# The first expert product in fp32 on two 64-row tiles, in place of fp16 high and low halves

## The reference

```python
x = x + ssm(_ln_c(x))            # 64->168 projection, state per image, layernorm over 128, 128->64
t = tokens(x)
t = t + moe0(_ln_t(t))           # 8 experts 64->128->64, exact gelu, two of them weighted per token
x = x + conv(_ln_c(x))           # channel groups of 8 and a 3x3 neighbourhood of the squares
t = t + moe1(_ln_t(t))           # 8 experts 64->256->64, weights: softmax over the two best

def moe(xf):                     # all experts are computed for all tokens
    for e in range(8):
        h = gelu(xf @ W1[e] + b1[e])
        out = out + w[:, e:e + 1] * (h @ W2[e] + b2[e])
```

## Time and profile before

| | |
|---|---|
| median of 3 runs | 723.12 us |
| span of the profiled execution (its own time) | 721.9 us |
| PE busy | 540.6 us (75%), 3010 instructions |
| DVE busy | 523.5 us (73%), 926 instructions |
| ACT busy | 377.9 us (52%), 440 instructions |
| POOL busy | 283.2 us (39%), 240 instructions |
| chain that ended last | DVE 39%, DMA 22%, PE 15% |

### The profile page before, as it was taken

How to read it: one execution, slowest core, us unless ns; L and a number is a source line. 1 busy time by engine, 2 the same in 40 slices (tenths; PEclk the granted TensorE clock), 3 DMA queues, 4 the chain that set the end, 5 groups by cost and what they waited for, 6 DMA issues and landing times.

```text
span 721.9 us, 8643 instructions
## 1 busy us (share of the span) xinstructions
PE 540.6 (75%) x3010; PEld 214.2 (30%) x3010; DVE 523.5 (73%) x926; ACT 377.9 (52%) x440; POOL 283.2 (39%) x240
## 2 busy tenths in 40 slices
PE   2314674589777988799778978798879786975776
PEld 1213223232323332343224323333333221321312
DVE  3266367868798979887998898889978796466312
ACT  2112712566566656756575657555766464543532
POOL 2122156034534453536362544365245433334013
PEclk9999975699999999999999999999999998998699
DMA  4500600063106230605041503350145005500240
GB/s 67 96 9 1 133 0 0 7 128 87 32 1 134 50 69 15 133 12 108 16 107 27 119 16 72 62 119 16 38 81 117 17 14 106 118 16 0 48 86 15
DMA packets 27834, 41.39 MB, mean 57 GB/s; under 512 B 11792, under 2 KB 19088, under 8 KB 27792
## 3 DMA queue, kind: packets, MB, share of 16 engines
q1 hardware_dynamic: 27152, 38.75, 26.2%
q0 software_dynamic: 640, 2.10, 1.0%
HBM read 38.22 MB, written 2.62 MB: 57 GB/s over the span
## 4 chain that ended last, share of the span: by engine, by line
DVE 39%; DMA 22%; PE 15%; issue 8%; POOL 7%; SPq 5%; ACT 4%; POOLq 0%; DVEq 0%; ACTq 0%
DMA WB<-w_scratch 18%; DVE nacc L1132 6%; PE yP L859 5%; PE hP L844 4%; SPq L402 3%; DMA w_scratch<-wTs 3%; DVE YW L1179 2%; POOL stat_c L486 2%; PE sA L760 2%; DVE xsplit L969 2%; PE sA L770 2%; DVE xcen_b L962 2%; POOL stat_b L486 2%; DVE xnrm L962 1%; DVE xnrm L957 1%
## 5 line engine op out<-in xcount | busy, mean ns | idle before, releaser
L691 ACT ACTIVATE H<-hP,b 128x1024 f32<-128x1024 f32 x192 | 209.2, 1110 | 82.6 <-PE hP L844 81.5
L859 PE MATMUL yP<-H,w 128*64 128x512 f32 x768 | 211.3, 632 | 21.3 <-DVE ACC L1179 19.3
L844 PE MATMUL hP<-xT,w 128*128 128x512 f16 x768 | 209.9, 399 | 4.3 <-ACT H L691 4.3
L556 POOL TENSOR_TENSOR ACC<-ACC,YW 128x512 f32<-128x512 f32 x96 | 125.6, 1313 | 194.6 <-DVE YW L1179 194.5
L844 PEld LDWEIGHTS hP<-xT,w 128*128 128x128 f16 x768 | 65.9, 101 | 145.8 <-issue 84.5
L1179 DVE SCALAR_TENSOR_TENSOR YW<-yP,b,WB 128x512 f32<-128x512 f32 x96 | 71.3, 744 | 34.2 <-PE yP L859 34.2
L859 PEld LDWEIGHTS yP<-H,w 128*64 128x64 f32 x768 | 40.1, 138 | 103.3 <-issue 89.0
L1132 DVE SCALAR_TENSOR_TENSOR nacc<-PAD,taps,nacc 128x256 f32<-128x256 f32 x112 | 60.5, 540 | 3.7
L1179 DVE SCALAR_TENSOR_TENSOR ACC<-yP,b,WB 128x512 f32<-128x512 f32 x32 | 23.1, 746 | 46.9 <-DMA WB<-w_scratch 46.9
L540 POOL TENSOR_SCALAR nrg<-nacc,go_col 128x512 f32<-128x512 f32 x8 | 12.6, 1574 | 68.9 <-ACT nacc L659 68.9
L584 ACT ACTIVATE xsq<-xcen 128x512 f32<-128x512 f32 x24 | 15.0, 626 | 36.1 <-DVE xcen L941 36.0
(11 more groups left out here) (144 smaller groups left out, 761.9 us busy)
## 6 DMA issues: line engine op xcount, KB each, us to landing
WB<-w_scratch SPq DMA_DIRECT2D x32, 1024.0 KB, 9.9
X<-in_x SPq DMA_DIRECT2D x8, 256.0 KB, 12.0
out<-X POOLq DMA_DIRECT2D x8, 256.0 KB, 2.8
H<-in_L_ffn_W SPq DMA_DIRECT2D x2, 512.0 KB, 6.2
H<-in_L_ffn_W SPq DMA_DIRECT2D x2, 256.0 KB, 4.2
w<-in_L_ffn_W SPq DMA_DIRECT2D x1, 512.0 KB, 4.8
w_scratch<-wTs SPq DMA_DIRECT2D x16, 32.0 KB, 1.8
w<-in_L_ffn_W SPq DMA_DIRECT2D x1, 256.0 KB, 4.1
```

What stands on the lines that cost most here:

```text
L556: pool.tensor_tensor(ACC[l][:, cols], ACC[l][:, cols], YW[:, u % 4, :], ALU.add).then_inc(summed, 1)
L691: nc.scalar.activation(H[:, s % RING, :], hP[s % 2][:, :], ACT.Gelu, bias=b1[l][:, e * ch + c:e * ch + c + 1], scale=1.0 / WS)\
L844: mm = nc.tensor.matmul(hP[s % 2][:, hf * HALF:(hf + 1) * HALF], w1[l][:, sp, w, :], xT[l][g % 2][:, hf * HALF:(hf + 1) * HALF], start=(sp ...
L859: mm = nc.tensor.matmul(yP[hf][a * C:(a + 1) * C, :], w2[l][:, (2 * j + a) * ch + c, :], H[:, (2 * ch * j + 2 * c + a) % RING, hf * HALF:( ...
```

## The change

The inputs of the experts and of the gate stay fp32. The normalised tensors of b and d are not cast or split. PE turns two tiles of 128 tokens by 64 channels in one fp32 transpose of 128x128; four of them make xT, now 128x512: the channels of the even tiles on the partitions 0 to 63 and those of the odd tiles on 64 to 127. W1 is loaded by DMA as fp32 on both halves and not split. A slot has two fp32 matmuls, one over the rows 0 to 63 and one over 64 to 127, each into its own half of hP. The gate weights stand as a block diagonal, 8 columns for the upper and 8 for the lower half, and four fp32 matmuls make the logits. Tokens are thus in the order even tiles, odd tiles throughout a layer; the write of wgt and the residual additions take this into account by their access patterns. The loads of the experts' constants wait for the memsets of the gate weights.

The order is the same; eight transposes become four and wait for the normalisation itself, four matmuls of hP become two, and sixteen of the gate four. The core of the diff:

```diff
--- before.py
+++ after.py
...
@@ -168,11 +168,10 @@
         alog = sb("alog", [P, HEADS])
         expa = sb("expa", [P, HEADS])
         dpar = sb("dpar", [P, HEADS])
-        gw_f = [sb(f"gw_f{l}", [P, E]) for l in range(2)]
-        gw = [sb(f"gw{l}", [P, 2, E], F16) for l in range(2)]
+        gw = [sb(f"gw{l}", [P, 2 * E]) for l in range(2)]
         gb = [sb(f"gb{l}", [P, E]) for l in range(2)]
         NC = [E * c for c in CHUNKS]
-        w1 = [sb(f"w1_{l}", [P, 2, NC[l], P], F16) for l in range(2)]
+        w1 = [sb(f"w1_{l}", [P, NC[l], P]) for l in range(2)]
         w2 = [sb(f"w2_{l}", [P, NC[l], C]) for l in range(2)]
         b1 = [sb(f"b1_{l}", [P, NC[l]]) for l in range(2)]
         b2 = [sb(f"b2_{l}", [P, PAIRS]) for l in range(2)]
@@ -200,12 +199,10 @@
         xcen_b = sb("xcen_b", [P, T, C])
         xsq_b = sb("xsq_b", [P, T, C])
         xnrm_b = xcen_b
-        xsplit_b = sb("xsplit_b", [P, T, 2 * C], F16)
         xsplit = sb("xsplit", [P, T, 2 * C], F16)
-        xsplit2 = sb("xsplit2", [P, T, 2 * C], F16)
         stat = {L: sb(f"stat_{L}", [P, 4, T]) for L in "anbcd"}
         xTa = sb("xTa", [P, TOK], F16)
-        xT = [[sb(f"xT{l}_{i}", [P, TOK], F16) for i in range(2)] for l in range(2)]
+        xT = [[sb(f"xT{l}_{i}", [P, HALF]) for i in range(2)] for l in range(2)]
         proj = sb("proj", [P, T, PROJ])
         ctS = sb("ctS", [64, HALF])
         zdt = sb("zdt", [P, 5, T, HEADS])
...
@@ -405,29 +404,27 @@
             load("in", both_halves(win_f, W_in) + [(dtb[:, :], rep(dt_bias)), (alog[:, :], rep(A_log))])
             load("out", [(wout_f[:, :], W_out), (gam_col[:, :], ln_gamma.rearrange("(c o) -> c o", o=1)),
                          (bet_col[:, :], ln_beta.rearrange("(c o) -> c o", o=1)), (dpar[:, :], rep(D_param))])
-            load("experts0", both_halves(gw_f[0], g0_w) + [(gb[0][:, :], rep(g0_b))] + [
-                (w1_f[half * C:half * C + C, 0:NC[0] * P].rearrange("d (e h) -> d e h", e=E),
-                 m0_W1.rearrange("e d h -> d e h")) for half in range(2)] + [
+            sp.wait_ge(zeroed, 7 + E)
+            load("experts0", gate_halves(0, g0_w) + [(gb[0][:, :], rep(g0_b))] + [
+                (w1[0][half * C:half * C + C, :, :], m0_W1.rearrange("e d h -> d e h")) for half in range(2)] + [
                 (b1[0][:, :], m0_b1.rearrange("e h -> h e")), (w2[0][:, :, :], m0_W2.rearrange("e h f -> h e f"))] + [
                 (b2[0][half * C:half * C + C, :], m0_b2.rearrange("(j a) f -> a f j", a=2)[half])
                 for half in range(2)])
             load("conv1", both_halves(taps, gamma_s.rearrange("a b c o -> c (a b o)"))
                  + both_halves(nbias, beta.rearrange("(c o) -> c o", o=1))
                  + both_halves(go_col, gamma_out.rearrange("(c o) -> c o", o=1)) + [(bo_rep[:, :], rep(beta_out))])
-            sp.wait_ge(zeroed, 2)
             gk = gamma_k.rearrange("a b i o -> (a b i) o")
             for half in range(2):
                 for grp in range(8):
                     r = half * C + grp * 8
                     sp.dma_start(mix[r:r + 8, r:r + 8], gk[:, grp * 8:grp * 8 + 8]).then_inc(mix_loaded, 16)
-            load("experts1", both_halves(gw_f[1], g1_w) + [(gb[1][:, :], rep(g1_b)),
+            load("experts1", gate_halves(1, g1_w) + [(gb[1][:, :], rep(g1_b)),
                  (b1[1][:, :], m1_b1.rearrange("e (c h) -> h (e c)", h=P)),
                  (w2[1][:, :, :], m1_W2.rearrange("e (c h) f -> h (e c) f", h=P))] + [
                 (b2[1][half * C:half * C + C, :], m1_b2.rearrange("(j a) f -> a f j", a=2)[half])
-                for half in range(2)])
-            for half in range(2):
-                sp.dma_start(w1_f1[half * C:half * C + C, :].rearrange("d (e h) -> d e h", e=E),
-                             m1_W1.rearrange("e d h -> d e h")).then_inc(w1_loaded, 16)
+                for half in range(2)] + [
+                (w1[1][half * C:half * C + C, :, :].rearrange("d (e c) h -> d e (c h)", e=E),
+                 m1_W1.rearrange("e d h -> d e h")) for half in range(2)])
 
             def spread_weights(l, g):
 
...
@@ -689,7 +687,7 @@
                     c, a = r // 2, r % 2
                     e = 2 * j + a
                     nc.scalar.activation(H[:, s % RING, :], hP[s % 2][:, :], ACT.Gelu,
-                                         bias=b1[l][:, e * ch + c:e * ch + c + 1], scale=1.0 / WS)\
+                                         bias=b1[l][:, e * ch + c:e * ch + c + 1])\
                         .then_inc(gelu_done, 1)
 
             walk(moe, final, ab, cd, ACT_AT)
@@ -706,14 +704,23 @@
                     mm = nc.tensor.transpose(dst[:, t * P:(t + 1) * P], src(t), ident16[:, :])
                 mm.then_inc(tr[L].sem, 1)
 
+            def transposes_in_pairs(L, g, dst, after):
+
+                for sm, v in after:
+                    pe.wait_ge(sm, v)
+                for b in range(4):
+                    mm = nc.tensor.transpose(dst[:, b * P:(b + 1) * P], LN[L]["n"][:, 2 * b:2 * b + 2, :],
+                                             ident32[:, :])
+                mm.then_inc(tr[L].sem, 1)
+
             def gate_product(l, g, ps, src):
+
                 if g == 0:
-                    pe.wait_ge(prep, PREP[f"experts{l}"])
+                    pe.wait_ge(loaded[f"experts{l}"], 16 * LOADS[f"experts{l}"])
                 pe.wait_ge(trS[("b", "d")[l]].sem, trS[("b", "d")[l]].at(g))
-                for t in range(T):
-                    for s in range(2):
-                        mm = nc.tensor.matmul(ps[:, t * E:(t + 1) * E], src[:, t * P:(t + 1) * P], gw[l][:, s, :],
-                                              start=(s == 0), stop=(s == 1))
+                for b in range(4):
+                    mm = nc.tensor.matmul(ps[:, b * 2 * E:(b + 1) * 2 * E], src[:, b * P:(b + 1) * P], gw[l][:, :],
+                                          start=True, stop=True)
                 mm.then_inc(gmm[l].sem, 1)
 
             def gate_transpose(l, g, ps):
@@ -785,8 +792,7 @@
                                                   wout[:, n % 2, :], start=(n == 0), stop=(n == 3))
                     mm.then_inc(omm.sem, 1)
                 elif k == "turn_b":
-                    transposes16("b", g, sA16, lambda t: xsplit_b[:, t, :],
-                                 [a_read(k, g), (ln_lo["b"].sem, ln_lo["b"].at(g))])
+                    transposes_in_pairs("b", g, sA, [a_read(k, g), (ln_v["b"].sem, ln_v["b"].at(g))])
                 elif k == "gate":
                     pe.wait_ge(*a_read(k, g))
                     gate_product(0, g, sA, xT[0][g % 2])
...
@@ -839,11 +844,11 @@
                     j, r = s // (2 * ch), s % (2 * ch)
                     c, a = r // 2, r % 2
                     w = (2 * j + a) * ch + c
-                    for sp in range(2):
-                        for hf in range(2):
-                            mm = nc.tensor.matmul(hP[s % 2][:, hf * HALF:(hf + 1) * HALF], w1[l][:, sp, w, :],
-                                                  xT[l][g % 2][:, hf * HALF:(hf + 1) * HALF],
-                                                  start=(sp == 0), stop=(sp == 1))
+                    for hf in range(2):
+
+                        rows = slice(hf * C, (hf + 1) * C)
+                        mm = nc.tensor.matmul(hP[s % 2][:, hf * HALF:(hf + 1) * HALF], w1[l][rows, w, :],
+                                              xT[l][g % 2][rows, :], start=True, stop=True)
                     mm.then_inc(h_ready, 1)
 
                 unit = y_unit(m, s)
@@ -891,7 +896,9 @@
             v.memset(neg_half[:, :], -0.5).then_inc(zeroed, 1)
             for e in range(E):
                 v.memset(iota_m8[:, e:e + 1], float(e - E)).then_inc(zeroed, 1)
-            dve.wait_ge(zeroed, 5 + E)
+            for l in range(2):
+                v.memset(gw[l][:, :], 0.0).then_inc(zeroed, 1)
+            dve.wait_ge(zeroed, 7 + E)
 
             def split(dst_hi, dst_lo, src):
 
...
@@ -918,15 +923,7 @@
                 elif which == "bias":
                     dve.wait_ge(bias_mm, 1)
                     did(v.tensor_copy(out_bias[:, :], sC[:, 0:C]))
-                elif which == "experts0":
-                    dve.wait_ge(loaded["experts0"], 16 * LOADS["experts0"])
-                    split(gw[0][:, 0, :], gw[0][:, 1, :], gw_f[0][:, :])
-                    split(flat[0][:, 0], flat[0][:, 1], w1_f[:, 0:NC[0] * P])
-                elif which == "experts1":
-                    dve.wait_ge(loaded["experts1"], 16 * LOADS["experts1"])
-                    split(gw[1][:, 0, :], gw[1][:, 1, :], gw_f[1][:, :])
-                    dve.wait_ge(w1_loaded, 32)
-                    split(flat[1][:, 0], flat[1][:, 1], w1_f1[:, :])
+                elif which == "conv1":
                     dve.wait_ge(loaded["conv1"], 16 * LOADS["conv1"])
                     did(v.tensor_scalar(nbias[:, :], nbias[:, :], 1e-6, None, ALU.add))
                 assert steps[0] == PREP[which]
@@ -961,12 +958,9 @@
```

(22 more changed lines are left out.)

35 lines of the change are left out of this document (16 added, 19 removed).

## The result

The changed kernel takes 717.09 us as the median of 20 runs (709.39 to 724.27), the kernel before 723.9 us (20 runs, 722.27 to 730.02). The ratio is 0.9864, 95% interval 0.9843 to 0.9885: 1.4% faster, some 10 us by the ratio and 7 by the medians. The forecast was 707.5 us, with a range of 697 to 719.

A forecast was written before the change was run, and what follows sets the result against it. No engine alone bounds it: DVE and DMA take turns. Span 721.9 - 7.7 (b) - 5.0 (d, steady) - 2.1 (d, last group) - 2.0 (start) + 1.2 (hP) = 706.3; median 1.2 above: 707.5 us, range 697 to 719.

The forecast's parts named there:

- the forecast's own case: Whole kernel: the summed terms hold, 707.5 us, within 702 to 713 us, chance 0.50.
- rival 3: Slow clock falls on the chain in piece 4 of every period: 8 us of gain back, 713 to 718 us, chance 0.10.
- Split of b: In piece 2, YW on DVE begins 1.1 us earlier without the split, in seven groups: 7.7 us gained.
- Piece 2: Steady period, first ACC of layer 1 to wgt of layer 0 (410.71 to 441.15): DVE instruction behind DVE instruction.
- hP in fp32: Two fp32 products of 64 rows per step: 1.06 us, 0.1 more; 12 times on the chain, 1.2 us lost.
- rivals 4 and 5: Row tiles of hP overlap partly (4: 718 to 726 us, chance 0.13) or run one after another (5: 880 us, 0.11).
- piece 4: Steady period, first ACC of layer 0 to next write of layer 1, 14.6 us: gains between 0.2 and 1.7 us.
- Start, -2.0: Start: W1 split of 5.0 us goes, transposes, evacuation and gate product of 3 us replace it: 2.0 us gained.
- Gate, transposes and evacuation: PE's transposes about equal, evacuation about 0.4 us less, gate about 0.4 us more: together zero, bounds +-0.5 us.
- d, steady: Split of d removed in five steady periods: piece 3 keeps its length, piece 4 gains 1.0 us each, 5.0 us.
- piece 3: Steady period, wgt to first ACC of layer 0 (441.15 to 456.77): set by DMA, removing d's split worth zero.
- Last group, -2.1: Last group: the split of d stands on the chain itself, 2.2 us, of which 2.1 go.

The follow-up runs named there:

- e2: The kernel before without the subtraction that makes the low part of b, the cast staying: 720.63 us, ratio 0.9925.
- e12: The changed kernel with only the first two of the four matmuls of each gate product: 711.07 us, ratio 0.9782.
- e4: The changed kernel with each of the four matmuls of the gate product made twice: 734.03 us, ratio 1.0135.
- e6: The changed kernel with the read of layer 0's expert weights (WB) cut to a tiny piece from the second group on: 696.61 us, ratio 0.9615.
- e10: The changed kernel with POOL's product Yd held until DVE has written Vs: 723.81 us, ratio 0.9977.
- e7: The changed kernel with nine fp16 matmuls, result unread, put in pauses of PE to keep it busy: 715.36 us, ratio 0.9828.

## Why the prediction was right, and where it was wrong

The direction and the range held; the point was some 7 to 10 us too low. The result lies outside the 702 to 713 us of the forecast's own case and within the 713 to 718 of rival 3, which had a chance of 0.10 and whose mechanism, more slow clock in every steady period, is not what the steady periods show. That the range took it in is in part luck.

By stretches, the profile has 12.3 us more than the 706.3 of the sum, in three nearly equal parts. Up to the write of layer 1, group 0, the terms give 3.1 us and 0.9 was lost; in the five periods they give 10.0 and 6.1 came; behind them they give 2.5 and 1.9 was lost.

- **Split of b, 7 x 1.1 us: right.** YW starts 1.67 us behind the start of the normalisation, 2.85 before: 1.18. Piece 2 is 31.5 to 30.3 us in the trace. Its subtraction alone (e2) gives 5 us.
- **hP in fp32, 1.06 us a step: right** in its size, 1.05. The rivals 4 and 5 fell: two row tiles run side by side as two column tiles do (1.05 us for both, 1.10 for one full product), even writing all 128 partitions each. The count of the steps was too low: the sum had one hP step on the chain in each piece 4, and the chain of the change at 452.11 to 467.78 has four, 0.4 us in place of 0.1. PE's busy time in the five periods rose from 319.1 to 339.8 us, 4.1 a period, where the sum had 2.4. The estimate of 1.3 times one product, worked out from the figure for four row tiles in the Trainium skill, TensorE: Matmul & The Clock Gate, packing section, does not hold for a pair here.
- **Start, -2.0: right in its result**, 72.49 instead of 74.47, with 3.7 us from the transposes to the end of the gate (63.61 to 67.34) where the sum had 3. It is lost again by 170 us.
- **Gate, transposes and evacuation, "together zero": the step that failed.** It took 0.4 us more for the gate and set it against the shorter evacuation. The product grew by 0.5 us at the full clock (0.56 to 1.06) and by 1.3 at half the clock, where it takes 1.82 to 1.87 us now and took this before, at a granted clock of 0.50:

```profile
671.58 0.58 PE sC L715 x16
```

  And it is not beside the path but on it, in the start, in nearly every piece 4 and in the last group. e12 prices half of it at 6 us, e4 a second one at 18. That is the larger part of the miss. The forecast had put a small figure on eight passes of few columns with no row behind it. The rows that were there show that few columns don't make the weight load shorter: in fp16 it takes 98 ns ahead of 8 columns (L715) and 101 ahead of 512 (L844). For fp32 it is 225 to 254 ns at L722, but 150 to 160 at L712 for the same shape, so what sets the pace of the gate product stays open.
- **d, steady, 5 x 1.0: too much, and by another route.** The forecast had DVE wait 4.4 us at ACC; it waits 1.81. Of the 3.7 us, 2.3 went into the zdt instructions beside POOL and 0.3 into a wait for ACT. The price of 3.7 us was that of the split beside POOL; the split by itself is 1.1. Piece 4 gained 1.8 us where the clock stayed high (12.80 us), 1.1, 0.5 and -0.3 in the three with one slow stretch, and lost 1.1 in the first, beyond both bounds; 2.1 us in five periods. That piece 3 is worth nothing was right in its result (e6), but the reason given, that WB sets it, was half of it: the path over Vs and PE is as long, and it is the one on the chain of before in all five periods.
- **Last group, -2.1: won in its place and lost beside it.** From the write of layer 1 for group 6 to that for group 7 it is 59.74 us before (618.35 to 678.09) and 59.34 after (614.44 to 673.78), 0.4 less. From the normalisation of d to gt the chain is 1.2 us shorter (6.90 to 5.71): the split is gone and the evacuation is 0.4 shorter, but the gate takes 1.87 us at half the clock where it took 0.58. Ahead of it, though, 0.9 were lost, between the write and the normalisation; which part of PE's work took them is open.

```profile
666.10 1.87 PE sC L722 x8
```

- **Rival 3**, the slow clock on the chain, came true in part: in the first two of the six pieces 4, and fully in e10. Single runs of the change spread over 15 us, those of before over 8. That this spread is the clock's doing was read from profiles of single runs, not shown by an experiment: e7, meant for it, stays unclear.

The terms that missed overlap (the gate is part of piece 4 and of the last group), so I don't add them.
